# Point-cloud window attention on one core: the gather stage with natural-order differences, 32-column strips, and the second order written by ScalarE

## The chip, the cores and the metric

The kernel runs on one core of one Trainium2 chip, as one launch. The engines of the core are TensorE (PE, with its weight loads shown apart as PEld), VectorE (DVE), ScalarE (ACT) and GpSimd (POOL); SyncE (SP) issues the DMAs, which sixteen DMA engines carry out. The metric is the device time of a launch in microseconds, lower is better, as a median of several runs.

## The reference

Three residual parts: a cross-attention over a point cloud (twice a layer of "window attention"), a Mamba-2 like mixer, and a feed-forward part. The change is inside the first. Cut to what matters there:

```python
def _window_inds(sorted_idx, k=10):          # 512 points in one of 4 sorted orders
    start = jnp.maximum(0, i - k // 2)
    end = jnp.minimum(N, i + k // 2 + 1)
    pos = jnp.minimum(start[:, None] + jnp.arange(k)[None, :], (end - 1)[:, None])
    return jnp.take(sorted_idx, pos, axis=1)
...
neigh = gather(feats, inds)                  # 10 neighbours of each point, 32 features
gf = jnp.concatenate([center, neigh - center], axis=-1)
allf = jnp.stack(per_method, axis=-1)[..., perm]     # 4 methods
x16 = x.astype(jnp.float16).astype(jnp.float32)      # rows of 256, in 8 heads of 32
scores = einsum(qh, qh) / sqrt(32); attn = softmax(scores)
fused = einsum(attn, qh) @ W_lin.T + b_lin
```

There are 16 batches of 512 points, 32 features and 4 sorted orders ("methods"), and the whole is done for two layers.

## The kernel before

The program is a list of stages one after the other, with a barrier between them. For each of the two layers they are: `fold_weights` (small), `gather_windows` (which the change rewrites), `window_attention` (the largest, unchanged but for the names of the tensors it loads), and `instance_norm`. `gather_windows` works on one batch at a time, in a software pipeline: `steps` (L454 to L464) runs `step` once per batch, and `at(j)` inside it is the batch that came j steps ago, so that an engine does different parts for different batches in one step. The order of instructions on an engine is the order of the code in its `step`.

For a batch b, with 128 partitions = 32 features c times 4 methods m:

- SP loads the features `fb` [32, 512] (L557). PE spreads them to 128 partitions (`pcen`, L640) and transposes them to tokens (`ptok`, L642).
- DVE splits `ptok` in a high and a low half, `t16` (L601) and `l16` (L603), and copies both, interleaved with zeros, into `FX` (L609), so that feature c of method m lies in column 4c + m of a 128-column weight. It builds sixteen 0/1 masks `onehot` (L614) out of the ranks.
- PE gathers: 64 multiplications with `FX` as weights and `onehot` as data into `pext` [128, 2, 283] (L654), the features in sorted order, with the ends of the windows repeated. ACT copies it to `ext` (L688), and copies the centres from `pcen` to `cen16` and `cen` (L681, L682).
- DVE makes the differences `QT` (`window_rows`, L535 and L543): twelve instructions for the three points n of a subgroup, the subgroup index s innermost, so each reads `ext` and `cen` three elements (12 bytes) apart and writes `QT` in the order (group, position x, subgroup s).
- ACT turns `QT` into the second order (group, s, x) in `QS` (L672), one instruction of 5760 elements that reads 15 elements (30 bytes) apart.
- SP stores `QT` (L562), `cen16` (L564) and, a step later, `QS` (L569) to the DRAM tensors `q16`, `c16` and `r16`. Each store is one DMA over 128 partitions, with packets of 960 bytes (of 90 for the centres). In the traces `q16` and the others are named scratch_q, scratch_c and scratch_r.

In a step b, DVE does masks(b) and then differences(b-2); ACT does QS(b-3), cen(b), ext(b-1); PE does the spreading of b and the gathering of b-1; SP loads fb(b), stores QT and centres of b-3, and QS of b-4. There are four buffers of `QT`, `cen` and `ext`, two of `QS`, `FX` and `onehot`. The counter `q_out[k]` counts the stores out of buffer k: DVE's differences and ACT's cen of batch b wait until all stores of batch b-4 have landed.

`window_attention` then loads for each pair of groups `q16` in four DMAs of 32 partitions (QX, L800), and `r16` in one of 128 (QM, L802). After the second layer, `join_features` loads its `f_j` in four rounds of five DMAs (L1107 to L1111): 32 partitions x 4 x 512 words into partitions 0 to 31, 32 x 4 x 507 into 32 to 63, 64 x 4 x 507 into 64 to 127, and two small ones, and behind them `lat_j` over all 128 partitions (L1113). PE multiplies a round when it has landed (L1125).

Of the kernel before, what the change touches and what calls it, by code (L numbers as in the profile page):

```python
# [6 lines left out]
F32 = mybir.dt.float32  # L7
# [23 lines left out]
EXT = LEAD * K + N + HALF - 1  # L31
# [438 lines left out]
def gather_windows(nc, io, scratch, layer, feats, runs, perm, rank):  # L470


    with ExitStack() as ctx:
# [16 lines left out]
        FX = sb("FX", [128, 2, 2, M * NT * 128], F16)  # L490
# [4 lines left out]
        qt = sb("QT", [128, 4, GROUPS * GC], F16)  # L495
        QT = qt[:, :, :].rearrange("p b (g x s) -> p b g x s", g=GROUPS, x=32)
        qs = sb("QS", [128, 2, GROUPS, SUBS, 32], F16)
# [4 lines left out]

        const_in = sem("const_in")
        zeroed = sem("zeroed")
        fx_zeroed = sem("fx_zeroed")
# [4 lines left out]
        fx_ready = sem("fx_ready")  # L512
# [7 lines left out]
        QV = 12  # L520
# [3 lines left out]
        def window_rows(eng, k, n, sem_):  # L524

            last = None
            for g0, g1, s0, s1 in ((0, 1, 2, SUBS), (1, GROUPS - 1, 0, SUBS),
                                   (GROUPS - 1, GROUPS, 0, NSUB - SUBS * (GROUPS - 1))):
                base = 44 + n + GP * g0 + PTS * s0
                at = ext[:, k, base:base + 1]  # L530
                ctr = cen[:, k, GP * g0 + PTS * s0 + n:GP * g0 + PTS * s0 + n + 1]
                G, U = g1 - g0, s1 - s0
                src = bass.AP(at.tensor, at.offset, [at.ap[0], [GP, G], [1, K], [PTS, U]])
                cbc = bass.AP(ctr.tensor, ctr.offset, [ctr.ap[0], [GP, G], [0, K], [PTS, U]])
                last = eng.tensor_tensor(QT[:, k, g0:g1, n * K:(n + 1) * K, s0:s1], src, cbc, ALU.subtract)  # L535
                last.then_inc(sem_, 1)

            U = 2 if n < LEAD - PTS else 1
            at = ext[:, k, K * n:K * n + 1]
            ctr = cen[:, k, n:n + 1]  # L540
            src = bass.AP(at.tensor, at.offset, [at.ap[0], [1, K], [K * PTS, U]])
            cbc = bass.AP(ctr.tensor, ctr.offset, [ctr.ap[0], [0, K], [PTS, U]])
            eng.tensor_tensor(QT[:, k, 0, n * K:(n + 1) * K, 0:U], src, cbc, ALU.subtract).then_inc(sem_, 1)  # L543

        @block.sync
        def _(sp):
# [4 lines left out]
            def step(k, at):  # L551
                k0 = k
                if at(0):
                    b, _ = at(0)
                    sp.wait_ge(f_used, b + 1)
                    for s0, n0, n1 in runs:
                        sp.dma_start(fb[:, k % 2, n0:n1], feats[:, bass.ds(b, 1), s0:s0 + n1 - n0]  # L557
                                     .rearrange("c b n -> c (b n)")).then_inc(f_in[k % 2], 16)
                if at(3):
                    (b, _), k = at(3), (k - 3) % 4  # L560
# [3 lines left out]
                    sp.dma_start(scratch["c16"][bass.ds(b * GROUPS, GROUPS), :, :].rearrange("g p x -> p g x"),  # L564
                                 cen16[:, k, :].rearrange("p (g x) -> p g x", g=GROUPS)).then_inc(q_out[k], 16)
                if at(4):
                    (b, _), k4 = at(4), k0 % 4
                    sp.wait_ge(q_turned, b + 1)
                    sp.dma_start(scratch["r16"][bass.ds(b * GROUPS, GROUPS), :, :].rearrange("g p x -> p g x"),  # L569
                                 qs[:, k4 % 2, :, :, :].rearrange("p g s x -> p g (s x)")).then_inc(q_out[k4], 16)  # L570

            steps(sp, step, B, 4)
            for k in range(4):
                sp.wait_ge(q_out[k], 48 * (B // 4) + 48)

        @block.gpsimd
        def _(pool):
            nc.gpsimd.memset(cen[:, :, :], 0.0).then_inc(zeroed, 1)
            nc.gpsimd.memset(cen16[:, :, :], 0.0).then_inc(zeroed, 1)
            nc.gpsimd.memset(qt[:, :, :].bitcast(F32), 0.0).then_inc(zeroed, 1)  # L580
            pool.wait_ge(zeroed, 3)
            for k in range(4):
                pool.sem_inc(q_out[k], 48)

        @block.vector
        def _(dve):
            v = nc.vector
            for hl in range(2):
                v.memset(FX[:, hl, :, :].bitcast(F32), 0.0).then_inc(fx_zeroed, 1)
            dve.wait_ge(const_in, 48)  # L590
            dve.wait_ge(fx_zeroed, 2)
# [3 lines left out]
            def step(k, at):  # L595
                if at(0):
                    (b, _), h = at(0), k % 2

                    dve.wait_ge(f_used, b + 3)
                    dve.wait_ge(gathered, b + 1)  # L600
                    v.tensor_copy(t16[:, h, :], ptok[:, h, 0:NT * C]).then_inc(t16_ready, 1)  # L601
# [3 lines left out]
                    dve.wait_ge(l16_ready, b + 3)  # L605
                    for hl, src in enumerate((t16, l16)):
                        fx = FX[:, hl, h, 0:1]
                        dst = bass.AP(fx.tensor, fx.offset, [fx.ap[0], [NT * 128 + 1, M], [M, NT * C]])
                        v.tensor_copy(dst, src[:, h, :].unsqueeze(1).to_broadcast([128, M, NT * C]))\  # L609
                            .then_inc(fx_ready, 1)  # L610

# [5 lines left out]
                if at(2):  # L617
                    (b, i), k = at(2), (k - 2) % 4
# [3 lines left out]
                    dve.wait_ge(q_out[k], i * 48 + 48)  # L622
                    for n in range(PTS):
                        window_rows(v, k, n, q_v)
# [1613 lines left out]
```

## Time and profile before

| | us |
|---|---|
| median of 3 runs | 3178.42 (3177.49 to 3185.07) |
| the profiled execution | 3193.7, span 3191.9 |
| PE busy / DVE / ACT / POOL | 2304.3 / 2343.3 / 1750.2 / 1045.3 |
| gather stage, layer 1 / 2 | 289.5 / 293.7 |
| window attention, layer 1 / 2 | 563.0 / 580.5 |
| DMA share over the span (q1) | 39.9% |

The span is the time between the first and the last instruction of one execution, under the profiler. Busy times count what an engine executes, not its waits. Two kinds of reading are used below: the busy time of each engine and of the DMA engines in a stretch of the span (windows), and the instructions in order of time (timeline), where a bracket tells how long the engine was idle before the instruction and what ended the wait.

### The profile page before, as it was taken

To read this page: it belongs to the slowest core of one execution; us is meant where nothing else is said; L and a number is where in the kernel's file an instruction comes from. 1 tells how busy PE (TensorE), PEld (TensorE's weight loads), DVE (VectorE), ACT (ScalarE), POOL (GpSimd) and SP (SyncE) were. 2 spreads that over 40 slices of the span, in tenths; PEclk is the share of its full clock that TensorE was granted. 3 is DMA by queue.
4 is the path that set the end of the run, shared out by engine and by line. 5 is a ranking of instruction groups with operands and counts; after the bars stand their busy time and mean duration, and the time that the engine had idled before them with its cause. 6 is when DMAs were issued, how large, how long until landed. Compare 5 with 4: busy or idle time off the path is not lost. (4 is left out here: it accounts for less than half of the span.)

```text
span 3191.9 us, 101454 instructions
## 1 busy us (share of the span) xinstructions
PE 2304.3 (72%) x37716; PEld 1694.6 (53%) x37716; DVE 2343.3 (73%) x4333; ACT 1750.2 (55%) x3096; POOL 1045.3 (33%) x985
## 2 busy tenths in 40 slices
PE   0122777499999935763999999902979988888867
PEld 0111555488888834443999999801344444444432
DVE  8566899476777748895777777725568988888875
ACT  0575587665666623876888888801434444444432
POOL 0001000366666621001666666600023333333321
PEclk9999888576788867886999999955989999999987
DMA  0774488743434432888333333271122222222210
GB/s 31 157 181 97 109 211 199 179 94 91 94 92 96 95 29 67 198 201 203 86 86 88 90 86 88 65 77 52 52 70 67 73 69 69 66 69 69 63 54 13
DMA packets 395931, 309.43 MB, mean 97 GB/s; under 512 B 147101, under 2 KB 347875, under 8 KB 395744
## 3 DMA queue, kind: packets, MB, share of 16 engines
q1 hardware_dynamic: 395744, 306.68, 39.9%
q8 instruction: 149, 2.44, 0.3%
q14 instruction: 38, 0.31, 0.0%
HBM read 200.96 MB, written 105.62 MB: 96 GB/s over the span
## 5 line engine op out<-in xcount | busy, mean ns | idle before, releaser
L839 PE MATMUL pQ<-QM,QX 128*128 128x64 f16 (+1 forms) x5760 | 753.4, 236 | 0.0
L837 PE MATMUL pQ<-neigh_lo,QX 128*128 128x32 f16 (+1 forms) x5760 | 736.9, 213 | 0.0
L837 PEld LDWEIGHTS pQ<-neigh_lo,QX 128*128 128x128 f16 x5760 | 726.5, 163 | 5.6
L839 PEld LDWEIGHTS pQ<-QM,QX 128*128 128x128 f16 x5760 | 719.2, 160 | 1.6
L929 POOL TENSOR_TENSOR Dm<-Sc,mx 128x450 f32<-128x450 f32 x384 | 366.0, 953 | 301.2 <-DVE mx L891 301.0
L936 POOL TENSOR_TENSOR Ap<-E,R 128x450 f32<-128x450 f32 x384 | 366.7, 955 | 96.6 <-DVE R L904 88.3
L672 ACT ACTIVATE QS<-QT 128x5760 f16<-128x5760 f16 x32 | 345.7, 10803 | 35.1 <-DVE QT L543 29.3
L955 ACT ACTIVATE Sc<-pQ 128x450 f32<-128x450 f32 x384 | 211.4, 551 | 234.8 <-PE pQ L839 228.2
L891 DVE TENSOR_REDUCE mx<-Sc 128x15 f32<-128x450 f32 x384 | 239.2, 623 | 124.4 <-ACT Sc L955 102.5
L654 PE MATMUL pext<-onehot,FX 128*128 128x283 f16 x2048 | 295.8, 313 | 17.3 <-issue 17.3
L1836 POOL TENSOR_TENSOR MT<-cb,decay 128x512 f32 (+1 forms) x128 | 185.3, 1466 | 333.7 <-DVE zero_m L1734 266.8
L961 ACT ACTIVATE Vs<-pQ 128x480 f32<-128x480 f32 (+1 forms) x384 | 293.9, 765 | 0.0
L654 PEld LDWEIGHTS pext<-onehot,FX 128*128 128x128 f16 x2048 | 216.3, 107 | 89.5 <-issue 17.5
L535 DVE TENSOR_TENSOR QT<-ext,cen 128x130 f16<-128x130 f32 (+2 forms) x288 | 256.6, 956 | 9.0 <-issue 9.0
L900 DVE STREAM_TRANSPOSE AT<-Ap 128x480 f32<-128x480 f32 x384 | 257.4, 670 | 4.1 <-POOL Ap L936 3.8
L832 PE MATMUL pQ<-maskR,maskL 128*128 128x160 f16 (+1 forms) x960 | 155.7, 263 | 139.1 <-DMA QM<-scratch_r 98.8
L1713 ACT ACTIVATE hid<-cv_m 128x512 f32<-128x512 f32 x64 | 40.3, 630 | 390.5 <-DVE cv_m L1369 390.5
L895 DVE TENSOR_REDUCE Z<-E 128x15 f32<-128x450 f32 x384 | 234.8, 612 | 0.0
L910 DVE TENSOR_REDUCE hmax<-Hs 128x450 f32 (+1 forms) x144 | 89.5, 622 | 189.1 <-ACT junk L980 189.1
L974 ACT ACTIVATE E<-Dm 128x450 f32<-128x450 f32 x384 | 223.5, 582 | 0.0
L864 PEld LDWEIGHTS pH<-AT,Vs 128*32 128x32 f32 x17280 | 189.9, 116 | 54.8 <-issue 34.8
L377 ACT ACTIVATE sign<-diff,lcol 128x512 f16<-128x512 f32 (+3 forms) x256 | 139.8, 548 | 137.1 <-DVE diff L345 136.9
(341 smaller groups left out, 4162.9 us busy)
## 6 DMA issues: line engine op xcount, KB each, us to landing
scratch_q<-QT SPq DMA_DIRECT2D x32, 1440.0 KB, 6.0
scratch_r<-QS SPq DMA_DIRECT2D x32, 1440.0 KB, 12.5
QX<-scratch_q SPq DMA_DIRECT2D x768, 60.0 KB, 1.9
QM<-scratch_r SPq DMA_DIRECT2D x192, 240.0 KB, 2.8
hall<-scratch_hi SPq DMA_DIRECT2D x16, 1024.0 KB, 9.5
lall<-scratch_lo SPq DMA_DIRECT2D x16, 1024.0 KB, 14.7
Wg<-in_in_proj SPq DMA_DIRECT2D x64, 256.0 KB, 2.7
Wh<-in_in_proj SPq DMA_DIRECT2D x64, 256.0 KB, 2.8
```

Of the source, the lines that this page charges most:

```text
L535: last = eng.tensor_tensor(QT[:, k, g0:g1, n * K:(n + 1) * K, s0:s1], src, cbc, ALU.subtract)
L654: last = nc.tensor.matmul(pext[:, h, e, 0:H2], FX[:, hl, h, mt * 128:(mt + 1) * 128], onehot[:, h, mt, e * H2:(e + 1) * H2], start=n == 0, ...
L672: nc.scalar.activation(qs[:, k3 % 2, :, :, :], QT[:, k3, :, :, :].rearrange("p g x s -> p g s x"), ACT.Copy).then_inc(q_turned, 1)
L837: nc.tensor.matmul(pQ[:, p, u // PB, o + 32:o + BW], qx[u], W["neigh_lo"][:, 0:O], start=False, stop=True, skip_group_check=True)
L839: last = nc.tensor.matmul(pQ[:, p, u // PB, o:o + BW], qx[u], qm[u], start=False, stop=True, skip_group_check=True)
L891: v.tensor_reduce(mx[:, p, :], valid(Sc[:, p, :]), X, ALU.max).then_inc(max_ready, 1)
L895: v.tensor_reduce(Z[:, p, :], valid(E[:, p, :]), X, ALU.add).then_inc(summed, 1)
L900: v.transpose(AT[:, k5 % NA, :], A[:, k5 % ND, :]).then_inc(turned, 1)
L929: nc.gpsimd.tensor_tensor(valid(Dm[:, p, :]), valid(Sc[:, p, :]), mx[:, p, :].unsqueeze(2).to_broadcast([128, SUBS, PTS * K]), ALU.subtrac ...
L936: nc.gpsimd.tensor_tensor(valid(A[:, p, :]), valid(E[:, p, :]), R[:, p, :].unsqueeze(2).to_broadcast([128, SUBS, PTS * K]), ALU.mult).then ...
L961: nc.scalar.activation(like(Vs[:, kv % RV, :], O, O), blocks(p, 32, O), ACT.Copy).then_inc(vs_ready, 1)
L974: nc.scalar.activation(valid(E[:, p, :]), valid(Dm[:, p, :]), ACT.Exp, scale=32.0 ** -0.5).then_inc(exped, 1)
```

## The change

It rewrites `gather_windows` in these points. Line numbers of the changed kernel are in the order listings.

- **Partitions.** Method m's features now lie in partitions 32m to 32m + 31 (`rep` is tiled and no longer repeated). The gather needs no `FX`: its weights are the 32 columns of `t16` or `l16`, and each of the 64 multiplications writes one strip of 32 partitions of `pext`. `FX`, its memsets, its copies and its semaphores go.
- **Stores.** The DRAM tensors keep their partition order c * 4 + m, so each store is split in four, one per strip of 32 partitions: four of `QT`, four of `cen16`, four of `QS`, twelve per batch in place of three.
- **Differences.** `ext` gets one more block of ten elements (576 in place of 566) so that all subgroups have the same address rule. One DVE instruction makes 171 x 30 differences in the order (s, n, j), j innermost and adjacent, a second one of 2 x 30 overwrites the first rows after it. `QT` is then in what was the second order.
- **The second order.** ACT writes `QS` from `QT`: it reads 30 adjacent elements and writes them 15 elements apart, 5400 in all. `QS` needs a memset now (POOL's fourth), and ACT waits for it before its first instruction.
- **Places in the pipeline.** Differences move from batch b-2 to b-1, QS from b-3 to b-2 and to the end of ACT's step; the copy t16 moves from DVE to ACT. SP's steps stay: QT of b-3, QS of b-4.
- `window_attention` loads QX from `x16` (QS) and QM from `q16` (QT), in the layouts that it had.

SP in the loop before, from the load of one batch to the load of the next; scratch_q is stored from QT, scratch_c from the centres, scratch_r from QS (ISA and REGISTER_ALU rows are waits and address sums):

```order
L557 DMA fb<-scratch_f 32x512
L561 ISA
L562 ISA
L562 DMA scratch_q<-QT 128x12x480
L564 ISA
L564 DMA scratch_c<-cen 128x12x45
L569 DMA scratch_r<-QS 128x12x480
L555 REGISTER_ALU
```

SP in the loop now, the last strip of QT and centres and the four of QS, ahead of the next load:

```order
L544 DMA scratch_q<-QT 32x12x480
L545 ISA
L545 DMA scratch_c<-cen 32x12x45
L552 ISA
L552 DMA scratch_x<-QS 32x12x480
L552 ISA
L552 DMA scratch_x<-QS 32x12x480
L552 ISA
L552 DMA scratch_x<-QS 32x12x480
L552 ISA
L552 DMA scratch_x<-QS 32x12x480
```

Ahead of these stand three more pairs of QT and centre strips: the three stores of a batch have become twelve, in the same place of SP's queue. ACT in the loop before, with its waits (t, cen, ext and QS as above):

```order
L672 ACTIVATE QS<-QT 128x5760 [waits q_out1_gw1,q_v_gw1]
L677 ISA [waits q_out2_gw1]
L678 REGISTER_ALU [waits q_v_gw1]
L681 ACTIVATE cen<-pcen 128x5 [waits f_used_gw1]
L682 ACTIVATE cen<-pcen 128x5
L681 ACTIVATE cen<-pcen 128x507
L682 ACTIVATE cen<-pcen 128x507
L688 ACTIVATE ext<-pext 128x566 [waits q_v_gw1,gathered_gw1]
```

And now:

```order
L650 ACTIVATE t<-ptok 128x128 [waits gathered_gw1,f_used_gw1]
L652 ISA [waits q_out1_gw1]
L654 ACTIVATE cen<-pcen 128x5 [waits q_v_gw1]
L655 ACTIVATE cen<-pcen 128x5
L654 ACTIVATE cen<-pcen 128x507
L655 ACTIVATE cen<-pcen 128x507
L661 ACTIVATE ext<-pext 128x576 [waits q_v_gw1,gathered_gw1]
L665 REGISTER_ALU
L667 ACTIVATE QS<-QT 128x12x15x30 [waits q_out1_gw1,q_v_gw1]
```

QS has moved behind ext, and the copy t, for which DVE waits, stands behind the QS of the step before. DVE of a batch now is one row of l, sixteen masks and two differences:

```order
L581 TENSOR_TENSOR l<-ptok,t 128x128 [waits t16_ready_gw1,gathered_gw1]
L585 TENSOR_SCALAR onehot<-place,rank 128x576 x16
L596 TENSOR_TENSOR QT<-ext,cen 128x171x30 [waits cen_ready_gw1,q_out1_gw1,ext_ready_gw1,zeroed_gw1]
L599 TENSOR_TENSOR QT<-ext,cen 128x2x30 [waits q_v_gw1]
```

The core of the diff:

```diff
-        FX = sb("FX", [128, 2, 2, M * NT * 128], F16)
-        QT = qt[:, :, :].rearrange("p b (g x s) -> p b g x s", g=GROUPS, x=32)
-        qs = sb("QS", [128, 2, GROUPS, SUBS, 32], F16)
+        QT = sb("QT", [128, 4, GROUPS, GC], F16)
+        qs = sb("QS", [128, 2, GROUPS * GC], F16)
+        QS = qs[:, :, :].rearrange("p b (g x s) -> p b g x s", g=GROUPS, x=32)
...
-                    sp.dma_start(scratch["q16"][bass.ds(b * GROUPS, GROUPS), :, :].rearrange("g p x -> p g x"),
-                                 QT[:, k, :, :, :].rearrange("p g x s -> p g (x s)")).then_inc(q_out[k], 16)
+                    for m in range(M):
+                        sp.dma_start(q16[m], QT[m * C:(m + 1) * C, k, :, :]).then_inc(q_out[k], 16)
+                        sp.dma_start(c16[m], cen16[m * C:(m + 1) * C, k, :].rearrange("p (g x) -> p g x", g=GROUPS))\
+                            .then_inc(q_out[k], 16)
...
+            nc.gpsimd.memset(qs[:, :, :].bitcast(F32), 0.0).then_inc(zeroed, 1)
...
-                    for n in range(PTS):
-                        window_rows(v, k, n, q_v)
+                    v.tensor_tensor(windows[0], rows(ext, k, LEAD * K + HALF - 1, (PTS, 1, 1), NSUB),
+                                    rows(cen, k, 0, (PTS, 1, 0), NSUB), ALU.subtract).then_inc(q_v, 1)
+                    dve.wait_ge(q_v, b * QV + 4 * QV + 1)
+                    v.tensor_tensor(windows[1], rows(ext, k, 0, (K * PTS, K, 1), 2),
+                                    rows(cen, k, 0, (PTS, 1, 0), 2), ALU.subtract).then_inc(q_v, 1)
...
+                            for m in range(M):
+                                last = nc.tensor.matmul(pext[m * C:(m + 1) * C, h, e, 0:H2],
+                                                        half[:, h, t * C:(t + 1) * C],
+                                                        onehot[:, h, m * NT + t, e * H2:(e + 1) * H2],
+                                                        start=n == 0, stop=n == 2 * NT - 1)
...
+                if at(2):
+                    (b, i), k2 = at(2), (k - 2) % 4
+                    act.wait_ge(q_v, b * QV + 5 * QV)
+                    act.wait_ge(q_out[(k2 + 2) % 4], (i + 1 + k2 // 2) * QO)
+                    nc.scalar.activation(QS[:, k2 % 2, :, 0:PTS * K, :].rearrange("p g x s -> p g s x"),
+                                         QT[:, k2, :, :].rearrange("p g (s x) -> p g s x", x=32)[:, :, :, 0:PTS * K],
+                                         ACT.Copy).then_inc(q_turned, 1)
```

## Rows read from the trace of the kernel before

**Rows 1.** Windows: the two gather stages, the two attention stages; first row: columns

```profile
core 0: us, PE busy (x) PEld busy (x) DVE busy (x) ACT busy (x) POOL busy (x), PEclk, DMA share, GB/s
305.00:594.50 289.50, 178.53 (x1120) 123.86 (x1120) 235.24 (x514) 199.82 (x96) 13.37 (x3) 0.81 0.72 175
1203.60:1497.30 293.70, 176.85 (x1120) 123.05 (x1120) 235.21 (x516) 199.82 (x96) 13.85 (x4) 0.77 0.70 173
595.00:1158.00 563.00, 507.79 (x12288) 476.90 (x12288) 395.31 (x819) 342.97 (x769) 365.65 (x387) 0.79 0.39 91
1497.50:2078.00 580.50, 551.90 (x18624) 526.20 (x18624) 425.20 (x869) 477.31 (x962) 366.86 (x387) 0.99 0.36 86
```

**Rows 2.** Timeline of one batch; start, us, engine, operation [idle before]

```profile
411.45 10.84 ACT L672 ACTIVATE QS<-QT 128x5760 f16<-128x5760 f16 x1
...
412.44 9.18 PE L654 MATMUL pext<-onehot,FX 128*128 128x283 f16 x64
412.54 0.29 DVE L601 CAST t<-ptok 128x128 f16<-128x128 f32 x1 [2.45 <-PE ptok L642]
...
414.32 4.49 DVE L614 TENSOR_SCALAR onehot<-place,rank 128x566 f16<-128x566 f16 x16
...
418.72 2.72 DVE L535 TENSOR_TENSOR QT<-ext,cen 128x130 f16<-128x130 f32 x3
...
424.15 0.18 ACT L681 ACTIVATE cen<-pcen 128x5 f16<-128x5 f32 x1 [1.87 <-DVE QT L535]
...
424.41 1.21 PE L640 MATMUL pcen<-fb,rep 32*128 32x512 f32 x2 [2.79 <-DMA fb<-scratch_f]
...
426.96 10.85 ACT L672 ACTIVATE QS<-QT 128x5760 f16<-128x5760 f16 x1 [1.06 <-DVE QT L543]
```

**Rows 3.** DMA issues, 400 to 480 us; GB/s in 40 slices of 587 to 594 us

```profile
scratch_r<-QS SPq DMA_DIRECT2D x6, 1440.0 KB, 12.2
scratch_q<-QT SPq DMA_DIRECT2D x5, 1440.0 KB, 6.0
scratch_c<-cen SPq DMA_DIRECT2D x5, 135.0 KB, 9.4
...
GB/s 71 77 137 368 362 357 357 384 362 362 346 357 340 357 340 346 379 373 362 379 357 362 329 307 313 335 181 49 33 16 0 0 0 0 0 0 0 0 0 0
```

**Rows 4.** join_features: DMA share and GB/s in 40 slices of 2134 to 2162; PE timeline

```profile
DMA  0017757999999999999999999999999999992000
GB/s 0 0 22 148 232 40 203 246 264 217 215 241 189 190 214 243 211 209 241 189 190 214 243 209 212 240 189 190 214 243 209 212 249 336 386 386 76 0 0 0
...
2147.83 1.94 PE L1125 MATMUL ph_j<-f_j,w_j 128*32 128x512 f32 x8 [2.87 <-DMA f_j<-scratch_f]
2152.73 1.93 PE L1125 MATMUL ph_j<-f_j,w_j 128*32 128x512 f32 x8 [2.96 <-DMA f_j<-scratch_f]
```

**Rows 5.** DVE's groups by form: times, busy and mean ns, idle before

```profile
L535 DVE TENSOR_TENSOR QT<-ext,cen 128x1500 f16<-128x1500 f32 x96 | 218.0, 2271 | 0.0
...
L1294 DVE TENSOR_TENSOR acc<-x_p,xin 128x2048 f32<-128x2048 f32 x1 | 2.3, 2293 | 0.0
```

**Rows 6.** ACT's groups by form

```profile
L672 ACT ACTIVATE QS<-QT 128x5760 f16<-128x5760 f16 x32 | 345.7, 10803 | 35.1 <-DVE QT L543 29.3 <-DMA scratch_r<-QS 3.2 <-DVE QT L535 2.6
...
L1978 ACT ACTIVATE W_f<-w_f 115x1536 f16<-115x1536 f32 x1 | 1.5, 1467 | 0.0
```

**Rows 7.** Timeline of PE: strip multiplications in the second attention stage

```profile
1600.93 0.37 PE L858 MATMUL pH<-CT,center_hi 128*32 128x450 f16 x4
1601.13 0.36 PE L858 MATMUL pH<-CT,center_lo 128*32 128x450 f16 x4
```

**Rows 8.** Timeline: start of the first gather stage; first instruction of the stage behind

```profile
308.83 9.70 POOL L580 MEMSET QT<- 128x11520 f32 x1
...
342.20 2.67 DVE L535 TENSOR_TENSOR QT<-ext,cen 128x130 f16<-128x130 f32 x3
...
350.37 0.41 SPq L562 DMA_DIRECT2D scratch_q<-QT  x1
...
594.54 1.70 POOL L918 MEMSET QX<- 128x1920 f32 x1 [276.00 <-POOLq L51]
```

More of the change, by code:

```diff
@@ L519, in gather_windows, with rows @@
         q_out = [sem(f"q_out{k}") for k in range(4)]
-        QV = 12
+        QV = 2
+        QO = 16 * 3 * M
         ctx.callback(clear, nc, used)
         block = ctx.enter_context(nc.Block())
[L524 to L543, printed above, removed]
+        def rows(tile, k, at, steps_, subs):
+            first = tile[:, k, at:at + 1]
+            return bass.AP(first.tensor, first.offset, [first.ap[0], [steps_[0], subs], [steps_[1], PTS], [steps_[2], K]])
         @block.sync
@@ L579, in _ @@
             nc.gpsimd.memset(cen16[:, :, :], 0.0).then_inc(zeroed, 1)
-            nc.gpsimd.memset(qt[:, :, :].bitcast(F32), 0.0).then_inc(zeroed, 1)
-            pool.wait_ge(zeroed, 3)
+            nc.gpsimd.memset(QT[:, :, :, :].bitcast(F32), 0.0).then_inc(zeroed, 1)
+            nc.gpsimd.memset(qs[:, :, :].bitcast(F32), 0.0).then_inc(zeroed, 1)
+            pool.wait_ge(zeroed, 4)
             for k in range(4):
-                pool.sem_inc(q_out[k], 48)
+                pool.sem_inc(q_out[k], QO)
         @block.vector
@@ L621, in step @@
                     dve.wait_ge(cen_ready, b + 3)
-                    dve.wait_ge(q_out[k], i * 48 + 48)
-                    for n in range(PTS):
-                        window_rows(v, k, n, q_v)
+                    dve.wait_ge(q_out[k], i * QO + QO)
+                    flat = QT[:, k, :, :].rearrange("p g x -> p (g x)").rearrange("p (s x) -> p s x", x=32)
+                    windows = [flat[:, 0:u, 0:PTS * K].rearrange("p s (n j) -> p s n j", n=PTS) for u in (NSUB, 2)]
+                    v.tensor_tensor(windows[0], rows(ext, k, LEAD * K + HALF - 1, (PTS, 1, 1), NSUB),
[3 more added lines that the diff above has]
+                                    rows(cen, k, 0, (PTS, 1, 0), 2), ALU.subtract).then_inc(q_v, 1)
             steps(dve, step, B, 4)
@@ L651, in step @@
                     for e in range(2):
-                        for n in range(2 * M * NT):
-                            hl, mt = n // (M * NT), n % (M * NT)
-                            last = nc.tensor.matmul(pext[:, h, e, 0:H2], FX[:, hl, h, mt * 128:(mt + 1) * 128],
-                                                    onehot[:, h, mt, e * H2:(e + 1) * H2],
-                                                    start=n == 0, stop=n == 2 * M * NT - 1)
+                        for n in range(2 * NT):
+                            half, t = (t16, l16)[n // NT], n % NT
+                            for m in range(M):
+                                last = nc.tensor.matmul(pext[m * C:(m + 1) * C, h, e, 0:H2],
+                                                        half[:, h, t * C:(t + 1) * C],
+                                                        onehot[:, h, m * NT + t, e * H2:(e + 1) * H2],
+                                                        start=n == 0, stop=n == 2 * NT - 1)
                     last.then_inc(gathered, 1)
@@ L797, in step @@
                     sp.wait_ge(projected, t + 2)
-                    src = scratch["q16"][bass.ds(t, 2), :, :].rearrange("g p x -> p g x")
+                    src = scratch["x16"][bass.ds(t, 2), :, :].rearrange("g p x -> p g x")
                     for h in range(4):
@@ L2158, in constants @@
     c["ident"] = np.eye(128, dtype=np.float32)
-    c["rep"] = np.repeat(np.eye(C, dtype=np.float32), M, axis=1)
+    c["rep"] = np.tile(np.eye(C, dtype=np.float32), (1, M))
     e = np.arange(EXT)
-    lead = np.minimum(e % K, e // K + LEAD)
-    place = np.where(e < LEAD * K, lead, np.minimum(e - LEAD * K, N - 1))
+    lead = np.where(e < LEAD * K, np.minimum(e % K, e // K + LEAD), -1)
+    place = np.where(e < (LEAD + 1) * K, lead, np.minimum(e - (LEAD + 1) * K, N - 1))
     c["place"] = np.tile(place.astype(np.float16), (128, 1))
```

65 lines of the change are left out of this document (24 added, 41 removed).

## The prediction

> **What bounds the kernel now.** I read the stages first. The change touches only the two gather stages, which take 289.5 and 293.7 us [rows 1], 583 of the 3191.9 us span. Each handles 16 batches, so the question is what one batch costs. In the timeline of one batch [rows 2] no engine is simply full: ACT's reordering copy QS starts at 411.45 and again at 426.96, a period of 15.5 us, and in it ACT works 13 us (10.84 for QS, the rest for cen and ext), DVE works from 412.54 to 426.7 with a wait of 2.45 us before, PE gathers for 9.2 us. The bracket of ACT's first cen names the DVE windows of four batches ago, DVE's names the small transposes on PE, PE's names a load of fb that stands in the queue behind the big stores. So three resources with 13 to 14 us of work each wait for one another in turn.
>
> The third is the DMA queue. Its share over the whole stage is 0.72 [rows 1]: 0.72 x 289.5 / 16 = 13.0 us of packets per batch. The two 1440 KB stores (2.95 MB) run at about 360 GB/s while nothing else is in the queue [rows 3], which is 8.2 us. The remaining 4.8 us are the rest: the 135 KB of centres, cut in 1536 packets of 90 bytes, that keep the following store waiting (landings of 6.0, 9.4 and 12.2 us), and the fb loads.
>
> **The change part by part.** *DVE.* Now per batch: 0.3 and 0.3 us for t and l, 1.4 for the two FX copies, 4.5 for sixteen masks, 8.0 for twelve difference instructions [rows 2], 14.2 in all. Gone are t (to ACT), and the FX copies. The differences become one instruction of 171 x 30 = 5130 elements and one of 60. Bounds for the big one: the dense rate, 2293 ns for 2048 elements, gives 1.05 to 1.12 ns per element and 5.5 us; today's strided form, 2271 ns for 1500, gives 1.41 (1.51 less some 0.15 us of start) and 7.4 us [rows 5]. Its inner run is ten adjacent elements, so I take 6 us. The small one is 0.2 to 0.3, the masks grow by 576/566 to 4.6. Sum 11 to 12.7 us, 11.5 taken.
>
> *ACT.* It gets t (0.3 us) and keeps cen and ext (2.2). QS today costs 10.8 us for 5760 elements read 30 bytes apart. Afterwards it reads in order and writes 30 bytes apart, 5400 elements. If only reading was slow, the dense rate of 1467 ns for 1536 elements [rows 6] gives 4.7 us; if writing costs the same, 10.1 us. No row shows ACT writing so; I take 7, the middle. Sum 7.2 to 12.6 us. QS moves one step earlier (batch b-2 in place of b-3), behind ext in the same step; queued behind it is the t of the next batch, for which DVE's l waits. That makes ACT and DVE start each batch together, at the period of the longer of them, which is at most 12.7 us.
>
> *PE.* 64 full-width multiplications of 283 columns, 9.2 us, become 64 of 32 output rows and 288 columns in four strips. Four such strips of 450 columns start together and the next four follow 0.20 us later [rows 7], so sixteen groups take 2 to 4 us. PE is not a bound today at 9.2, so this is worth nothing by itself.
>
> *The slack.* Windows and QS run one step earlier while SP keeps its steps, so a store is issued a whole step after its data is ready, and ACT's cen(b) waits for landings of b-4 that could be issued a step sooner. The ring of waits of [rows 2] loses its grip, and what remains is the longest single resource.
>
> *The DMA queue.* The same bytes in the same 960 and 90 byte packets, but twelve stores per batch in place of three, each from 32 partitions. SP's issue costs at least 0.37 us each, 5 us in all, under the period. What matters is the rate from 32 partitions. The nearest rows are the loads in join_features [rows 4]: four times 32-, 32- and 64-partition transfers, 1.05 MB a round (256 + 253.5 + 507 KB and small ones), at a spacing of 4.90 us (2147.83 to 2152.73). That is 214 GB/s with the queue full (share 9), and the 128-partition load straight behind it, lat_j, reaches 386 in the same line. Narrow transfers run at about 0.6 of the wide rate here. These are loads into SBUF with rows of 2 KB, ours are stores with rows of 960 bytes, so the step from one to the other is my choice. With 214: 2.95 MB / 214 = 13.8 us in place of 8.2. (The Trainium skill, page "SBUF — State Buffer", section "Door 1: The DMA port swizzle", says that 32 and also 64 neighbouring partitions reach 8 of the 16 DMA ports, some 218 GB/s against 436, and its summary asks for 128 partitions in one DMA: a rule against this change. By its 218 the stores would take 13.5 us, and the row at 214 agrees. By its reading at 1 MiB, 189, they would take 15.6.)
>
> Added to this is the rest of 4.8 us. In the join the small packets left hardly a trace in the round, because while one engine works on them its neighbour has the port; if that holds for the centres too they cost nothing, if not, all 4.8. Per batch 13.8 to 18.6 us; I take half, 2.5, and **16.3 us**. This exceeds ACT and DVE, so the queue sets the period.
>
> *Start and end.* ACT now waits for a fourth memset. POOL needs 9.70 us for 11520 words [rows 8], so 4.9 for the 5760 words of QS: t can start at 323.5 in place of 313. Then l 0.3, masks 4.6, gather(0) 4 to 5 (the clock is low), ext 0.7, differences 6.5: the first store at about 341, where the first difference starts only at 342.20 today and the first store at about 350. Then 16 periods, and 5 us for one gap at the start (batch 1's data is not ready) and the last landing. The stage ends at 341 + 16P + 5; it ends at 594.5 today [rows 8]. Twice the difference is 32P - 497 us: no change at P = 15.5, which is today's period, so the formula returns today's time.
>
> With P = 16.3 the kernel is 25 us slower: 3193.7 + 25 = 3218 for the profiled execution. That one was 15 us above the median of the runs shown (3178.4); on the median, **3203 us**.
>
> The attention stages read the same two orders from scratch (each tensor now holds the other's) with the same loads: nothing.
>
> **The rivals.**
>
> Narrow stores are not slow. The 4 x 60 KB loads of QX are also 32 partitions wide and today's page shows no complaint of them, and a store reads SBUF while the join's loads write it. Then the queue needs 13.0 us, DVE and ACT at most 12.7, and with a little coupling P = 13.2: 32 x 13.2 - 497 = -75, 3103 us. Against it: [rows 4].
>
> Narrow stores are slow but the centres hide behind them. P = 13.8 to 15, -55 to -17 us, about 3140 us (P = 14.3). For it: the join's small packets. Against: today the centres cost their full time beside wide stores.
>
> About the break-even, P = 15.2 to 15.8: within 10 us of today.
>
> ACT's strided writes cost more than its strided reads. It decides from QS = 13.8 us on (plus 2.5 makes 16.3). At twice today's price, 21.6 us, P = 24.1 and the kernel is 274 us slower, 3452 us. Only the absence of a row speaks for it.
>
> **How the numbers follow.** About 0.3% (9.5 us) is what a measurement of this kernel can tell from no change. Forecast, P above 15.8 by the queue: 0.46. ACT: 0.03. Break-even: 0.13. Centres hidden: 0.18. Narrow stores at full rate: 0.20. Slower by over 0.3%: 0.49; within: 0.13; faster: 0.38. The queue's ends 13.8 and 18.6 give -55 and +98 us; the range reaches below that to about -78 to take in the full-rate case, and above to +90: 3100 to 3268. The forecast's own range is 3187 to 3268.
>
> **What would show it.** In the profile after: stores of 360 KB from QT and QS with landings well above 6 us; a DMA share of 0.9 or more through both gather stages at some 180 to 190 GB/s on the mean, without slices near 360; SP's issues blocked most of the time; DVE busy 11 to 12.7 us per batch and idle else, its waits or ACT's naming the stores of QS; gather stages of about 302 and 306 us. The single difference instruction at 5.5 to 7.4 us, QS at 4.7 to 10.1. I am wrong if slices above 300 GB/s show up (the first rival: stages of 252 us), if DMA is full but the period is under 15.5 (the centres hide), or if ACT is busy throughout. Attention stages other than 563 and 581 us would be something I have not seen.

## The result, and the profile after

The changed kernel takes 3475.19 us (median of 4 runs, 3471.55 to 3476.98) against 3178.44 (3177.49 to 3185.07): a ratio of 1.0927, interval 1.0908 to 1.0946. It is 297 us slower, where 25 us slower was forecast, and lies above the whole range.

First the stages, as in [rows 1]: windows of the profile after, the two gather stages and then the two attention stages.

```profile
305.00:740.00 435.00, 90.24 (x1120) 52.85 (x1120) 166.22 (x304) 397.68 (x112) 16.36 (x5) 0.58 0.54 117
1355.00:1789.30 434.30, 90.22 (x1120) 52.25 (x1120) 166.23 (x304) 397.62 (x112) 15.82 (x3) 0.54 0.55 117
740.50:1303.50 563.00, 512.28 (x12168) 480.27 (x12168) 393.92 (x818) 341.43 (x765) 365.10 (x387) 0.78 0.38 91
1790.00:2370.50 580.50, 552.48 (x18624) 526.38 (x18624) 423.71 (x868) 476.86 (x961) 367.00 (x387) 0.99 0.35 86
```

Attention is what it was, 563.0 and 580.5 us. Each gather stage went from about 290 to 435 us, 286 us in all. The two profiled executions lie 283 us apart, so this is the whole loss. In it PE's busy time fell from 178.5 to 90.2 us and DVE's from 235 to 166, as meant, and the DMA share fell too, from 0.72 to 0.54. ACT alone rose, from 199.8 to 397.7 us.

The groups by line and form, with count, busy us, mean ns, and the idle time ahead of them:

```profile
L667 ACT ACTIVATE QS<-QT 128x5400 f16<-128x5400 f16 x32 | 748.3, 23445 | 2.8 <-DVE QT L599 2.8
...
L596 DVE TENSOR_TENSOR QT<-ext,cen 128x5130 f16<-128x5130 f32 x32 | 175.8, 5494 | 30.0 <-ACT ext L661 29.5 <-issue 0.5
...
L581 DVE TENSOR_TENSOR l<-ptok,t 128x128 f16<-128x128 f32 x32 | 9.3, 290 | 411.9 <-ACT t L650 411.9
```

QS was 10803 ns for 5760 elements [rows 6]. It is 23445 ns for 5400, 4.34 ns per element in place of 1.88, and in 32 instructions it waited 2.8 us in all. DVE waited 411.9 us for ACT's copy t. One batch in the timeline, where [rows 2] had a period of 15.5 us:

```profile
386.84 23.28 ACT L667 ACTIVATE QS<-QT 128x5400 f16<-128x5400 f16 x1
...
410.32 0.29 DVE L581 TENSOR_TENSOR l<-ptok,t 128x128 f16<-128x128 f32 x1 [14.42 <-ACT t L650]
410.53 4.55 DVE L585 TENSOR_SCALAR onehot<-place,rank 128x576 f16<-128x576 f16 x16
...
411.68 23.28 ACT L667 ACTIVATE QS<-QT 128x5400 f16<-128x5400 f16 x1
...
414.99 5.49 DVE L596 TENSOR_TENSOR QT<-ext,cen 128x5130 f16<-128x5130 f32 x1
420.52 0.22 DVE L599 TENSOR_TENSOR QT<-ext,cen 128x60 f16<-128x60 f32 x1
```

From one QS to the next are 24.84 us here; over the first stage QS starts from 337.2 to 705.9 us, fifteen periods of 24.58. ACT is busy all of it: DVE's 10.6 us of work stand between two waits for ACT. The DMA issues, with KB each and us to landing:

```profile
scratch_q<-QT SPq DMA_DIRECT2D x128, 360.0 KB, 4.6
scratch_x<-QS SPq DMA_DIRECT2D x128, 360.0 KB, 5.5
```

and what they moved, GB/s in 40 slices of 399 to 425 us, about one period:

```profile
GB/s 167 191 186 112 280 201 141 203 189 176 50 0 0 0 0 0 0 0 112 189 191 189 191 186 228 272 216 189 202 230 20 6 0 0 13 186 192 184 154 189
```

Most slices with stores in them stand at about 190 GB/s where wide ones ran at 360 [rows 3]; single ones reach 230 to 280. In between the queue is empty. So the narrow store is slow as forecast, a little below the 214 GB/s assumed, and costs nothing here, since ACT takes longer.

### The profile page after: what moved, and what is told of

Its sections match the earlier page's. It is cut to its first block and busy times, and to the rows that moved or that the text cites. A ratio compares the mean times of both kernels' runs of the same rounds, so it can differ in the third digit from the quotient of the medians.

```text
span 3474.9 us, 101760 instructions
## 1 busy us (share of the span) xinstructions
PE 2130.3 (61%) x37716; PEld 1557.7 (45%) x37716; DVE 2202.7 (63%) x3913; ACT 2145.1 (62%) x3128; POOL 1054.1 (30%) x987
## 5 line engine op out<-in xcount | busy, mean ns | idle before, releaser
L667 ACT ACTIVATE QS<-QT 128x5400 f16<-128x5400 f16 x32 | 748.3, 23445 | 2.8 <-DVE QT L599 2.8
L631 PE MATMUL pext<-onehot,t 128*32 128x288 f16 x1024 | 73.3, 437 | 521.5 <-DVE onehot L585 441.7
L631 PEld LDWEIGHTS pext<-onehot,t 128*32 128x32 f16 x1024 | 35.7, 138 | 540.0 <-DVE onehot L585 444.6
L581 DVE TENSOR_TENSOR l<-ptok,t 128x128 f16<-128x128 f32 x32 | 9.3, 290 | 411.9 <-ACT t L650 411.9
```

The source lines that it names most:

```text
L667: nc.scalar.activation(QS[:, k2 % 2, :, 0:PTS * K, :].rearrange("p g x s -> p g s x"), QT[:, k2, :, :].rearrange("p g (s x) -> p g s x", x ...
```

## The experiments

The theory W: ACT pays for 2-byte writes 30 bytes apart, whatever surrounds them. The rival C: ACT is slow because of its company (one dense DVE instruction, more transfers) or because of the pattern's holes. Beside it stood the forecast's own claim, that strips of 32 partitions store slowly (N) against "they don't" (F).

**The write undone.** Same elements, same tensors; only the side of the copy that steps is exchanged.

```diff
-nc.scalar.activation(QS[:, k2 % 2, :, 0:PTS * K, :].rearrange("p g x s -> p g s x"),
-                     QT[:, k2, :, :].rearrange("p g (s x) -> p g s x", x=32)[:, :, :, 0:PTS * K],
+nc.scalar.activation(QS[:, k2 % 2, :, 0:PTS * K, :],
+                     QT[:, k2, :, :].rearrange("p g (s x) -> p g x s", x=32)[:, :, 0:PTS * K, :],
```

> The changed kernel with one thing undone: ACT's turn now writes QS in its own order and reads QT with a step of 32 elements (64 bytes); same 5400 elements, same stores, same DVE. Theory W (the stepped write is what costs): the turn falls from 23.4 us to about 5400 x 1.88 ns = 10.1 us, ACT's batch to about 12 us, and the period is what the narrow stores need, about 2.95 MB / 190 GB/s = 15.5 us and up to 2 us of gaps: 16 to 17 us, total 3475 - 32 x (24.8 - 16.5) = 3210 us (3190 to 3240). Rival C (ACT is slow because it shares memory with DVE's one dense instruction and more transfers, or because the pattern has holes at 30 of 32): the turn stays at 20 us or more, the total within 1.5% of 3475.

Measured: 3199.18 us, ratio to before 1.0046 (1.0026 to 1.0066), where the changed kernel had 1.0927: 276 us less. QS by its group, and the window 400 to 520 us:

```profile
L667 ACT ACTIVATE QS<-QT 128x5400 f16<-128x5400 f16 x32 | 302.2, 9445 | 22.5 <-DMA scratch_x<-QS 20.1 <-DVE QT L599 2.3
...
400.00:520.00 120.00, 48.42 (x559) 26.98 (x557) 79.09 (x135) 86.91 (x51) 0.00 (x0) 0.60 0.88 197
```

9.45 us, and it now waits for landings. The periods are 15.7 and 16.2 us in the two stages, 15.9 on the mean, with the DMA share at 0.88 and 197 GB/s. This is the kernel that the forecast described. W stands, C falls.

**The write put into the kernel before.**

```diff
-nc.scalar.activation(qs[:, k3 % 2, :, :, :], QT[:, k3, :, :, :].rearrange("p g x s -> p g s x"),
+nc.scalar.activation(qs[:, k3 % 2, :, :, :].rearrange("p g s x -> p g x s"), QT[:, k3, :, :, :],
```

> The kernel before with one thing changed: ACT's turn reads QT in its own order and writes qs stepped by 32 elements (64 bytes); every value is the same. Theory W: the turn goes from 10.8 us to 5760 x 4.34 ns = 25.0 us, ACT's batch to about 27 us, the period from 15.5 to about 26.5 us, total 3178 + 32 x 11 = 3530 us (3480 to 3580). Rival C (the slowness belongs to the new pipeline, not to the write): the turn stays at 10 to 12 us and the total within 0.5% of 3178.

Measured: 3567.01 us, ratio 1.1214 (1.1185 to 1.1242); the period is 26.73 us. Its turn is written 64 bytes apart and not 30. One line in the old pipeline, with its twelve difference instructions and wide stores, brings the loss by itself:

```profile
L672 ACT ACTIVATE QS<-QT 128x5760 f16<-128x5760 f16 x32 | 817.7, 25584 | 11.7 <-DVE QT L543 11.7
```

**The price by itself.** Copies at the end of the kernel before, one after another, nothing beside them. The whole ran once (3337.9 us), so each price below is one reading.

```diff
+link(cp(st(w16, 15), st(src[:, :], 1)))      # ACT, 720 f16, written 15 elements apart
+link(cp(st(w16, 1), st(src[:, :], 15)))      # read 15 elements apart
+link(cp(turn_out.rearrange("p g x s -> p g s x"), rows_in))    # a batch's turn, written stepped
+link(cp(turn_out, rows_in.rearrange("p g s x -> p g x s")))    # the same, read stepped
```

> The kernel before, with copies at its end that run one after another with nothing else running: 128 partitions x 720 f16 elements, on ACT written with a step of 1, 2, 4, 8, 15, 16 and 32 elements or read so, f32 forms, some of them on DVE and GpSimd, and the turn of one batch (5400 elements) written stepped or read stepped on each. Theory W: on ACT 720 elements take 0.8 to 0.9 us dense, 1.4 to 1.6 us read stepped (1.88 ns each) and 3.2 to 3.4 us written with a step of 15 (4.34 ns each), the turn 23 us written and 10 us read stepped, with no neighbour at all. Rival C (contention): the stepped write costs alone no more than the stepped read. Open: at which step the price rises, whether it is of the write's bytes or of its elements, and whether DVE and GpSimd pay it too.

ACT's copies (min/median/max ns of the one instruction, then its start). In order: f16 written with a step of 1, 2, 4, 8, 15 and 32 elements; f16 read with a step of 4 and 8; written as f32 with a step of 2, 4 and 15; the turn of a batch written stepped, and read stepped:

```profile
L2190 ACT ACTIVATE w_pr<-src_pr x1: 802/802/802, 3208.6 to 3208.6; 128x720 f16<-128x720 f16 x1
L2190 ACT ACTIVATE w_pr<-src_pr x1: 1003/1003/1003, 3209.5 to 3209.5; 128x720 f16<-128x720 f16 x1
L2190 ACT ACTIVATE w_pr<-src_pr x1: 1795/1795/1795, 3210.5 to 3210.5; 128x720 f16<-128x720 f16 x1
L2190 ACT ACTIVATE w_pr<-src_pr x1: 3381/3381/3381, 3212.3 to 3212.3; 128x720 f16<-128x720 f16 x1
L2190 ACT ACTIVATE w_pr<-src_pr x1: 3241/3241/3241, 3215.7 to 3215.7; 128x720 f16<-128x720 f16 x1
L2190 ACT ACTIVATE w_pr<-src_pr x1: 3323/3323/3323, 3222.3 to 3222.3; 128x720 f16<-128x720 f16 x1
...
L2190 ACT ACTIVATE w_pr<-src_pr x1: 839/839/839, 3226.4 to 3226.4; 128x720 f16<-128x720 f16 x1
L2190 ACT ACTIVATE w_pr<-src_pr x1: 1467/1467/1467, 3227.3 to 3227.3; 128x720 f16<-128x720 f16 x1
...
L2190 ACT ACTIVATE w_pr<-src_pr x1: 840/840/840, 3232.6 to 3232.6; 128x720 f32<-128x720 f16 x1
L2190 ACT ACTIVATE w_pr<-src_pr x1: 1467/1467/1467, 3233.5 to 3233.5; 128x720 f32<-128x720 f16 x1
L2190 ACT ACTIVATE w_pr<-src_pr x1: 1415/1415/1415, 3235.0 to 3235.0; 128x720 f32<-128x720 f16 x1
...
L2190 ACT ACTIVATE w_pr<-src_pr x1: 22985/22985/22985, 3237.9 to 3237.9; 128x5400 f16<-128x5400 f16 x1
L2190 ACT ACTIVATE w_pr<-src_pr x1: 9322/9322/9322, 3260.9 to 3260.9; 128x5400 f16<-128x5400 f16 x1
```

The turn takes 22.99 us alone and 23.4 in the kernel: its company is worth 2%. A stepped read costs almost nothing up to 8 bytes (839 ns) and from 16 bytes on 1.8 times the dense copy. A stepped f16 write is dearer from a step of 4 bytes on (1003), doubles with the step (1795, 3381 ns) and stays at 3.2 to 3.4 us from 16 bytes on, 4 times the dense copy. The same steps in bytes written as f32 cost 840 and 1467, what a read costs. So it is the 2-byte element that makes a stepped write dear, not the distance alone. DVE and GpSimd pay too, for the turn written and read stepped:

```profile
3280.55 11.65 DVE L2181 COPY w_pr<-src_pr 128x5400 f16<-128x5400 f16 x1
3292.23 4.91 DVE L2182 COPY w_pr<-src_pr 128x5400 f16<-128x5400 f16 x1
...
3302.92 22.97 POOL L2161 COPY w_pr<-src_pr 128x5400 f16<-128x5400 f16 x1
3325.95 9.27 POOL L2162 COPY w_pr<-src_pr 128x5400 f16<-128x5400 f16 x1
```

(The Trainium skill, page "SBUF — State Buffer", section "Door 1: The DMA port swizzle", notes lines of 16 bytes, a penalty for each access that goes to a new one, and a free step of up to 8 elements for 16-bit types. The reads agree in kind, though 8 elements already cost 1467 ns against 839 for 4; the page does not tell writes from reads, and the writes pay about twice as much as the reads from 4 elements on.)

**ACT taken out, with narrow and with wide stores.** Two kernels on the changed one. Both leave out the second order, and the one with wide stores also leaves each store in the tile's partition order, so attention works on other numbers in both:

```diff
-nc.scalar.activation(QS[:, k2 % 2, :, 0:PTS * K, :]...
+nc.scalar.activation(QS[:, k2 % 2, 0, 0, 0:1], QT[:, k2, 0, 0:1], ACT.Copy).then_inc(q_turned, 1)
```

> The changed kernel with the second order left out: ACT copies one element of it, and the store of x16 sends what QS holds from its fill, so attention works on other numbers; the bytes stored and all waits stay. What bounds the gather stage once ACT is out of it. Theory N (stores from 32 partitions go at about 190 GB/s, as the slices of the changed kernel's trace hold): 15.5 us of transfer and up to 2 us of gaps, period 15.5 to 17.5 us, total 3475 - 32 x (24.8 - 16.5) = 3210 us. Rival F (they reach the full rate when nothing else holds them): period 11.5 to 13.2 us, total 3050 to 3105 us.

> The changed kernel with the second order left out (ACT copies one element of it) and each of its three stores made from all 128 partitions at once, in the partition order of the tile, so attention works on other numbers. Beside the run with narrow stores it gives the price of the strips. Theory N: stores at the full rate take about 8.2 us; the period is DVE's 11.5 us and its waits, 11.5 to 13 us, total 3475 - 32 x (24.8 - 12.2) = 3070 us. Rival F: the same as with narrow stores, within 0.5%.

Measured: 3200.26 us with strips (ratio 1.0050, 1.0032 to 1.0068) and 3071.34 with wide stores (0.9654, 0.9630 to 0.9678). Their windows of 400 to 520 us, strips first:

```profile
400.00:520.00 120.00, 47.96 (x556) 26.59 (x555) 80.32 (x144) 15.09 (x50) 0.00 (x0) 0.58 0.89 196
```

```profile
400.00:520.00 120.00, 51.24 (x623) 29.34 (x621) 94.53 (x156) 18.01 (x59) 0.00 (x0) 0.61 0.93 262
```

With strips it makes no difference whether ACT's turn takes 9.45 us or nothing (3199, 3200): the stores set the period of 15.9 us, at 196 GB/s. Wide stores give 12.0 us. The strips cost 129 us, 4.0 per batch, as soon as ACT is out of the way. N stands, F falls. Even with wide stores it is the queue that sets the period, and not DVE, as was expected: the DMA share is 0.93 while DVE works 94.5 of 120 us. At 360 GB/s [rows 3] the two big stores take 8.2 of these 12.0 us, which leaves 3.8 for the centres and the load of fb. Beside narrow stores it leaves 0.4: 15.9 less 15.5, for 2.95 MB at 190 GB/s. Both are estimates.

**The strips alone, in the kernel before, and why they are slow.** Each store is split in four, once by neighbours and once by taking every fourth partition:

```diff
+for m in range(M):
+    at0, at1 = m * 32, m * 32 + 32
+    sp.dma_start(scratch["q16"][..., at0:at1, :]..., QT[at0:at1, k, :, :, :]...)    # strips
...
+    sp.dma_start(scratch["q16"][..., m::M, :]..., QT[m::M, k, :, :, :]...)          # every fourth
```

> The kernel before with each of its three stores split in four of 32 partitions; the same bytes land in the same places. The price of the narrow store alone. Theory N: 2.95 MB per batch (360 KB x 4 x 2 plus the centres) at about 190 GB/s = 15.5 us; the period of 15.5 us, which ACT and DVE set now, becomes 15.5 to 18 us, total 3180 to 3260 us, and the slices of DMA show 180 to 200 GB/s. Rival F (narrow stores reach the rate of wide ones): the same within 0.3%, 3178 us.

> The kernel before with each of its three stores split in four, as in the run with strips, but each part takes every fourth partition and not 32 neighbours; sizes, counts and bytes are the same. Tells why a narrow store is slow. Theory P (32 neighbouring partitions reach only part of the ways out of the memory): the parts now spread over all partitions and run at the rate of a whole store, total within 0.4% of 3180 us. Rival I (twelve stores cost SyncE's queue and the engines more than three): 3242 us again, as with strips.

Measured: strips 3241.87 us, ratio 1.0203 (1.0173 to 1.0233); every fourth 3176.02 us, 0.9979 (0.9968 to 0.9990). The landings of each, and the window of 400 to 520 us, strips first:

```profile
scratch_q<-QT SPq DMA_DIRECT2D x128, 360.0 KB, 4.4
scratch_r<-QS SPq DMA_DIRECT2D x128, 360.0 KB, 5.5
...
400.00:520.00 120.00, 84.06 (x484) 56.28 (x483) 97.96 (x221) 86.32 (x43) 0.00 (x0) 0.80 0.82 187
```

```profile
scratch_q<-QT SPq DMA_DIRECT2D x128, 360.0 KB, 3.1
scratch_r<-QS SPq DMA_DIRECT2D x128, 360.0 KB, 4.0
...
400.00:520.00 120.00, 89.24 (x556) 61.61 (x555) 112.56 (x254) 99.21 (x49) 0.00 (x0) 0.84 0.68 209
```

Twelve stores in place of three cost nothing; rival I falls. What costs is that the 32 partitions are neighbours. The order in DRAM does not decide it: the changed kernel's strips go to every fourth row there, the strips here to neighbouring rows, and both are slow. This is what theory P says; its reason, fewer ways out of the memory, is inferred. The kernel before had a DMA share of 0.84 at 203 GB/s in the same window, so every fourth partition, with 0.68 at 209, even keeps the engines less busy than the three wide stores. No run puts such stores under the mixture below.

**Two queues.** The kernel with the read-stepped turn, where ACT issues the stores of x16, in another strip order than SyncE's.

```diff
+for m in (2, 3, 0, 1):
+    nc.scalar.dma_start(x16[m], QS[m * C:(m + 1) * C, k % 2, :, :, :]...).then_inc(q_out[k], 16)
```

> The run that undoes only the stepped write (turn read stepped), with one thing more: the four stores of x16 are issued by ACT, one step later and in the strip order 2, 3, 0, 1, so two queues empty different strips at the same time; SyncE keeps q16 and the centres. Theory P: two strips at once draw from twice as many partitions, up to about 360 GB/s together, the period falls from 16.0 us to ACT's, 12 us and what its issues take (up to 4 x 0.5 us, more if its queue is full), 12.5 to 14.5 us, total 3199 - 32 x 2.5 = 3120 us (3085 to 3150). Rival I (the sixteen engines are busy 89% of the time and take so long for each packet whatever feeds them): 3199 us within 0.5%.

Measured: 3209.71 us, ratio 1.0082 (1.0065 to 1.0099). The total lies in rival I's band (3199 us within 0.5%), but not for its reason. ACT's timeline (ACTq is its DMA issues):

```profile
402.98 9.51 ACT L669 ACTIVATE QS<-QT 128x5400 f16<-128x5400 f16 x1
412.67 5.88 ACTq L645 DMA_DIRECT2D scratch_x<-QS  x4
418.72 0.28 ACT L652 ACTIVATE t<-ptok 128x128 f16<-128x128 f32 x1 [6.23 <-issue]
```

The slices with both queues at work (4 us each, 380 to 540 us) show 270 to 285 GB/s, and the DMA share is 0.73 where it was 0.88, so two strips at once are faster than one, as P says. But four issues hold ACT for 5.9 us, where 2 were allowed, and ACT's 12 us become 17.5 here (16.9 and 16.4 on the mean of the stages). The gain was spent on the engine that had none to spare.

**A mixture that beats both.** FX, partitions and wide stores of before, the one difference instruction and the pipeline places of the changed kernel, the turn read stepped.

> A mixture: the partitions, the copies into FX and the three 128-partition stores of the kernel before, with the one DVE instruction and the earlier pipeline places of the changed kernel, and the turn read stepped and written in its own order. Theory W and N together: turn about 10.1 us, DVE about 14 us a batch at the most (5.5 differences, 4.6 masks, the FX copies of before and the wait for ACT), stores at the full rate, 8.2 us; period 12.5 to 15 us, total 3178 - 32 x (15.5 - 13.5) = 3115 us (3080 to 3165). If wide stores are no faster than narrow ones (rival F's contrary), it gives the total of the run that only undoes the write, within 10 us.

Measured: 3132.68 us, ratio 0.9831 (0.9804 to 0.9858). The window of 400 to 520 us, and waits in it (us in total, times, longest):

```profile
400.00:520.00 120.00, 93.19 (x614) 65.77 (x613) 103.49 (x189) 100.65 (x63) 0.00 (x0) 0.82 0.92 232
...
ACT ext L667 <- PE pext L638: 17.2, 4, 4.9
DVE l L583 <- ACT t L656: 15.1, 5, 3.8
```

The period is 13.1 us: ACT waits for PE's gather, which waits for DVE's masks, and DVE's l for ACT's t. It is 1.7% faster than before. It is 61 us slower than the run without the turn and FX, of which 1.1 us per batch (35 us) is period and some 12 us per stage (24 us) a later start (first QS of the first stage at 349.3 in place of 337.2 us).

**GpSimd helps.** In the mixture, GpSimd makes the FX copies and two of the twelve groups of the turn.

```diff
+nc.gpsimd.tensor_tensor(dst, same, zero16[...], ALU.add).then_inc(fx_ready, 1)
+nc.gpsimd.tensor_tensor(QS[:, k2 % 2, GA:GROUPS, 0:PTS * K, :], same, zero16[...], ALU.add).then_inc(q_pool, 1)
```

> The mixture with wide stores, with GpSimd, idle in this stage, taking the copies into FX (2 x 0.76 us of DVE) and two of the twelve groups of the turn. If the mixture's period of 12.75 us is DVE's and ACT's own work, as its rows read (DVE 12.4 us, ACT 12.1 us a batch), DVE falls to 10.9 us and ACT to 10.6 us, GpSimd has 2 x 1.5 + 2 x 0.8 = 4.6 us, and the period is 11 to 11.8 us, total 3133 - 32 x 1.3 = 3090 us (3070 to 3115). Rival: GpSimd's copies lie on the chain halves, FX, matmuls, ext, differences, and slow DVE at their shared port; then the period stays at 12.5 us or more and the total at 3125 us or more.

Measured: 3162.42 us, ratio 0.9940 (0.9922 to 0.9958), 30 us slower than the mixture; the period is 14.16 us. The timeline:

```profile
402.73 8.57 DVE L616 TENSOR_SCALAR onehot<-place,rank 128x576 f16<-128x576 f16 x16
402.89 1.39 POOL L584 TENSOR_TENSOR FX<-t,zero 128x512 f16<-128x512 f16 x1 [9.46 <-DVE l L612]
404.10 1.53 POOL L584 TENSOR_TENSOR FX<-l,zero 128x512 f16<-128x512 f16 x1
...
405.45 2.33 POOL L591 TENSOR_TENSOR QS<-QT,zero 128x900 f16<-128x900 f16 x1
```

The sixteen masks by themselves (min/median/max ns):

```profile
L616 DVE TENSOR_SCALAR onehot<-place,rank x16: 357/358/2228, 402.7 to 410.9; 128x576 f16<-128x576 f16 x16
```

DVE's sixteen masks took 4.55 us without GpSimd beside them and take 8.57 with it. 1.5 us of copies were moved away and 4.0 us of delay came back: the rival. The delay isn't spread over the masks: thirteen take 0.36 us as ever, and three take 1.44, 1.43 and 2.23 us, about as long as the three GpSimd instructions (1.39, 1.53, 2.33) that run then. The kernel before had one such case: its first copy into FX, while GpSimd's memset ran [rows 8] until 318.5 us, took 5.3 us, the later ones 0.75:

```profile
313.81 5.32 DVE L609 COPY FX<-t 128x512 f16<-128x512 f16 x1
```

**Wide stores from strips.** The partitions of the changed kernel, read-stepped turn, and stores over all 128 partitions of two groups; the second kernel also gives t back to DVE.

```diff
+for j in range(0, GROUPS, 2):
+    x16 = scratch["x16"][bass.ds(b * GROUPS + j, 2), :, :].rearrange("g p x -> (g p x)")\
+        .rearrange("(c m x) -> m c x", m=M, c=C)
+    sp.dma_start(x16, QS[:, k % 2, j:j + 2, :, :].rearrange("p g x s -> p (g x s)")).then_inc(q_out[k], 16)
```

> The changed kernel with both of its dear forms replaced and all else kept: the turn is read stepped and written in order, and each store takes all 128 partitions of two groups, six for each of q16, x16 and the centres, into scratch tensors whose rows hold the two groups side by side (the loads of attention read them so). Theory: both terms were of the form and not of the work. Turn 9.46 us, ACT 12.0 us a batch, DVE 10.6 us, eighteen stores that SyncE issues in about 0.6 us each, 10.8 us, 8.2 us of transfer. Period 12.0 to 13 us, total 3199 - 32 x 3.6 = 3085 us (3060 to 3110). Rival (the number of stores costs as in the narrow ones, the rate stays near 190 GB/s): 16 us, 3199 us within 0.5%.

> The same with one more thing undone: DVE makes the high half t16 again and ACT doesn't. Of ACT's 12.0 us a batch 0.28 goes, DVE has 10.9 us. If ACT's own work sets the period this gives 32 x 0.28 = 9 us less than the run beside it, 0.2 to 0.4% faster; if DVE's wait for ACT's copy was on the chain it gives up to 25 us; if the stores set it, nothing.

Measured: 3768.84 and 3763.31 us, ratios 1.1838 (1.1816 to 1.1860) and 1.1821 (1.1799 to 1.1843), far from every number given. The window of the first one, 400 to 540 us, and GB/s in its 40 slices:

```profile
400.00:540.00 140.00, 25.51 (x280) 13.97 (x280) 43.52 (x82) 49.23 (x30) 0.00 (x0) 0.53 0.27 94
...
GB/s 88 87 89 88 99 115 99 99 91 86 87 87 88 99 99 113 99 91 87 88 88 88 90 99 113 99 100 89 87 87 87 87 97 99 113 99 95 87 87 88
```

The queue is never empty, and yet only a quarter of the engines' time is used (0.27 in the row). Most slices stand at 88 GB/s, a quarter of the wide rate; the mean is 94. Seen from DRAM the store's slowest dimension is m, of size 4. (The Trainium skill, page "DMA: Bandwidth & Descriptors", section "Rules for kernel authors", says that an outermost dimension smaller than 16 keeps the whole transfer on at most as many engines. That is 4 of 16, and the share and the rate both agree; no run here varies the size of that dimension, so the cause is argued and not shown.) The period is 32.8 us, so the second kernel tells nothing of t: the stores set it.

## Why the prediction was wrong

**The step that failed** is the term for ACT's QS. It was given as "7.2 to 12.6 us" for ACT's whole batch, from 4.7 us (only reading is slow) to 10.1 ("if writing costs the same"), with 7 taken, and "No row shows ACT writing so". It measured 23.4 us. The lower end came from a dense row and the upper end from the price of the stepped read; nothing in the profile says that a write can't cost more than a read. One row of before even hinted that it does, though on DVE. The copies into FX write f16 8 bytes apart and take 1.56 ns per element:

```profile
L609 DVE COPY FX<-l 128x512 f16<-128x512 f16 x32 | 25.6, 799 | 0.0
```

The dense masks take 0.65 (369 ns for 566 elements), which is another operation. On the upper end of 10.1 us rested the next sentence, that ACT and DVE have a period of "at most 12.7 us", and so the forecast that the queue sets the period. The bounds were bounds of the rows and not of the operation.

**The rival had the mechanism and nearly its size.** It put the point of decision at QS = 13.8 us, a price of 21.6 us, P = 24.1 and 3452 us. Measured: 23.4, 24.6 and 3475 us. It was given a chance of 0.03, because "only the absence of a row speaks for it". For an operation that 32 periods may wait for, and no row at all, that was too little, and the range left it out. (Its upper end of +90 us lies even below the +98 of the queue's own upper end.)

**The formula** held: 32 x 24.58 - 497 = +290 us, measured +297 (+283 between the profiled executions). It was set to return today's time at P = 15.5, one period read off the timeline; the periods of before are 15.0 and 15.4 on the mean of the stages, for which it gives -11, a small error. Its start was right (t at 321.4 for 323.5 us, the first store at 337 for 341).

**The queue** was right, and hidden. With the write undone the kernel takes 3199 us where 3203 was forecast, at a period of 15.9 us for 16.3; against its own runs of before that is 14 us slower, where 25 was forecast. That it comes so near is partly luck, since inside this term two errors cancel: the stores run at 190 GB/s and not at the 214 of the loads [rows 4], which makes 15.5 us of the 2.95 MB, and the centres add about 0.4 us and not 2.5. The rival of full rate falls (slices near 190). That of the hidden centres had the mechanism, slow stores and centres that cost next to nothing beside them, and falls only as priced, since it kept the 214. The reason that was given for it, a neighbour that has the port meanwhile, no run tests. (The Trainium skill, page "SBUF — State Buffer", section "Door 1: The DMA port swizzle", reads 189 GB/s at 1 MiB for 32 partitions. By that estimate the stores take 15.6 us, and the slices agree.)

**DVE** was 10.6 us for 11.5, with the difference instruction at 5.49 us, the dense end of 5.5 to 7.4. This is under the stated 11 to 12.7, because the sum was off: its lowest terms (0.3, 4.6, 5.5, 0.2) add up to 10.6. Likewise the terms given for today's DVE add up to 14.5 us and not 14.2. **PE** took 4.0 us (four groups of sixteen from 415.13 to 419.16 us, at a granted clock of 0.50, the 1.2 GHz level) for 2 to 4. **Attention** did not move.

**What would show it**: "if ACT is busy throughout" was named as what makes the forecast wrong, and it is what the profile shows.

## What to carry to other kernels

Where a copy must change the order of 2-byte elements, let it read stepped and write in order: exchanging the two sides of one instruction was worth 276 us here. A bound taken from the nearest row is only a bound if the row is the same kind of access; a term without a row on the path that repeats deserves a wide end and a chance, or a second way to do the work that needs no such term. When splitting a store, keep the parts spread over all partitions, and beware of a slowest dimension of 4 in DRAM. Before giving work to an idle engine, check what its instructions do to the busy one's that run at the same time: GpSimd's held up DVE's here.

## What the runs showed of the hardware that was not expected

- ACT's f16 writes with a step of 16 bytes or more take 4.5 to 4.7 ns per element (3207 to 3381 ns for 720) and 4.3 in a whole turn (22985 for 5400), its reads 2.0 (1467 ns for 720), its f32 writes 2.0; GpSimd's turn behaves the same (22.97 and 9.27 us), DVE's is half as long (11.65 and 4.91).
- DVE's difference with overlapping windows of ten in its source ran at 1.07 ns per element, the rate of a dense instruction.
- DVE's sixteen f16 masks took 8.57 in place of 4.55 us with GpSimd beside them; three of them took all of the delay, each about as long as the GpSimd instruction beside it.
- A store of every fourth partition landed in 3.1 us where one of 32 neighbours took 4.4.
- Stores whose slowest dimension had size 4 moved 88 to 115 GB/s (94 on the mean) at a DMA share of 0.27.
- Split in every fourth partition, the stores kept the DMA share at 0.68 for 209 GB/s, where three wide ones had 0.84 for 203.
